# A sequence of four layers on one core: z's high part ahead of the decay, and one tile's y and z a step earlier

## The reference

```
proj = norm(x) @ in_proj_w.T                 # gate (8192), x/B/C (8192 + 2 * 8 * 128), dt (128)
x, B, C = silu(causal_conv(x/B/C, 4 taps));   dt = softplus(dt + dt_bias)
per head h of 128 (64 channels each, 16 heads share a B and a C), in chunks of 128 tokens:
  L[t, s] = exp(cumsum(A dt)[t] - cumsum(A dt)[s]) for s <= t, else 0
  y[t] = sum_s (C[t] . B[s]) L[t, s] dt[s] x[s]  +  exp(cumsum)[t] * C[t] . state(chunk before)  +  D x[t]
y = y * rsqrt(mean(y^2) + eps) * norm_w * silu(gate);   x = x + y @ out_proj_w.T
```

## Time and profile before

| | |
|---|---|
| median of 3 runs | 1723.9 us (1722.81 to 1726.0) |
| the profiled execution | 1723.37 us, span 1721.7 us |
| PE busy | 1668.5 us (97%) |
| ACT, DVE, POOL busy | 1272.1 (74%), 1220.4 (71%), 756.3 us (44%) |
| mean granted clock of PE | 0.989 |
| chain that ended last | PE 80%, DVE 5%, ACT 2% |

### The profile page before, as it was taken

How to read it: one execution, slowest core, us unless ns; L and a number is a source line. 1 busy time by engine, 2 the same in 40 slices (tenths; PEclk the granted TensorE clock), 3 DMA queues, 4 the chain that set the end, 5 groups by cost and what they waited for, 6 DMA issues and landing times.

```text
span 1721.7 us, 27317 instructions
## 1 busy us (share of the span) xinstructions
PE 1668.5 (97%) x9616; PEld 1380.5 (80%) x9616; DVE 1220.4 (71%) x1940; ACT 1272.1 (74%) x2205; POOL 756.3 (44%) x800
## 2 busy tenths in 40 slices
PE   6998898999999999999999999999999999999998
PEld 5877677888888888888888888888888888888777
DVE  6885595767676777677766876776767676767784
ACT  4532249796888688878887888888878888788851
POOL 3662123543444444444444445344444444444570
PEclk9999999999999999999999999999999999999999
DMA  5220325232233233232333332323322323332311
GB/s 190 92 68 1 116 61 166 88 111 80 79 125 106 78 98 113 86 112 87 112 95 110 90 115 87 118 63 119 102 94 94 111 88 105 94 111 76 112 65 49
DMA packets 98567, 166.50 MB, mean 97 GB/s; under 512 B 11616, under 2 KB 49888, under 8 KB 96768
## 3 DMA queue, kind: packets, MB, share of 16 engines
q1 hardware_dynamic: 98432, 164.75, 30.2%
HBM read 158.43 MB, written 6.29 MB: 96 GB/s over the span
## 4 chain that ended last, share of the span: by engine, by line
PE 80%; DVE 5%; ACT 2%; issue 1%; DVEq 0%; ACTq 0%
PE bank L210 15%; PE bank L212 15%; PE bank L211 14%; PE bank L2048 7%; PE bank L2049 7%; PE bank L2014 7%; PE bank L2052 7%; PE bank L2034 4%; PE bank L2000 3%; PE bank L2098 1%; DVE m_xc L1708 1%; DVE m_y L1787 1%; ACT m_mt L1464 1%; DVE m_y L1777 1%; DVE m_gate L1708 0%
## 5 line engine op out<-in xcount | busy, mean ns | idle before, releaser
L210 PE MATMUL bank<-xh,w_h 128*128 128x512 f32 x1152 | 462.6, 402 | 4.2 <-DVE m_xc L1708 3.7
L212 PE MATMUL bank<-xh,w_l 128*128 128x512 f32 x1152 | 452.1, 392 | 0.0
L211 PE MATMUL bank<-xl,w_h 128*128 128x512 f32 x1152 | 448.8, 390 | 0.0
L1372 POOL TENSOR_TENSOR m_z_l<-m_zg,m_z_h 128x512 fp32r<-128x512 f32 x128 | 175.3, 1370 | 514.2 <-ACT m_z_h L1512 514.2
L1464 ACT ACTIVATE m_mt<-m_mt,m_unit 128x128 f32<-128x128 f32 x1024 | 312.2, 390 | 0.0
L1354 POOL TENSOR_TENSOR w_l<-w_raw,w_h 128x512 fp32r<-128x512 f32 x144 | 187.2, 1300 | 248.2 <-ACT w_h L1431 248.2
L1719 DVE TENSOR_TENSOR x<-x,bank 128x512 f32<-128x512 f32 x128 | 87.7, 685 | 248.6 <-PE bank L2052 248.6
L1708 DVE SCALAR_TENSOR_TENSOR m_xc<-bank,m_par_conv,m_xc 128x1020 f32<-128x1020 f32 (+2 forms) x192 | 244.5, 1273 | 14.7 <-ACT m_xc L1443 10.1
L212 PEld LDWEIGHTS bank<-xh,w_l 128*128 128x128 f32 x1152 | 216.4, 188 | 47.9
L210 PEld LDWEIGHTS bank<-xh,w_h 128*128 128x128 f32 x1152 | 217.1, 188 | 46.0 <-issue 5.5
L211 PEld LDWEIGHTS bank<-xl,w_h 128*128 128x128 f32 x1152 | 217.3, 189 | 41.9
(11 more groups left out here) (282 smaller groups left out, 2899.9 us busy)
## 6 DMA issues: line engine op xcount, KB each, us to landing
m_mt<-ncs_rows SPq DMA_DIRECT2D x128, 512.0 KB, 5.1
w_raw<-w_in SPq DMA_DIRECT2D x144, 256.0 KB, 2.7
m_wo_raw<-w_out_in SPq DMA_DIRECT2D x64, 256.0 KB, 4.1
m_e<-ecs_rows SPq DMA_DIRECT2D x128, 128.0 KB, 3.5
a_wo_raw<-wo_in SPq DMA_DIRECT2D x8, 1024.0 KB, 4.9
x<-x_in SPq DMA_DIRECT2D x8, 256.0 KB, 4.3
a_wq_raw<-wq_in SPq DMA_DIRECT2D x8, 256.0 KB, 3.1
x_saved<-x SPq DMA_DIRECT2D x1, 2048.0 KB, 8.8
```

Source lines behind the costliest of these rows:

```text
L210: nc.tensor.matmul(out, ah, bh, start=first, stop=False)
L211: nc.tensor.matmul(out, ah, bl, start=False, stop=False)
L212: return nc.tensor.matmul(out, al, bh, start=False, stop=last)
L1372: nc.gpsimd.tensor_tensor(z_l[:, s % 2, :, :], zg[:], f(z_h[:, s % 2, :, :]), ALU.subtract).then_inc(zl_ready, 1)
```

## The change

Two things are moved, and no instruction is added or removed.

1. In paired steps with t = 1, ACT makes Square and z's high part of tile s - 1 right after `wo_high`, ahead of the decay of tile s + 2.
2. Tile 7 of the last group (`made_last`) gets its y, z, Square, high and low part and its squares' sums at the end of step 7 of that group, its own step, no longer in step 8: on DVE after the mask of tile 9, on ACT after the Silu (ahead of step 8's eviction), on POOL ahead of the x of the chunk's end. SP's load of e for tile 11 moves with it.

```diff
         if not own(kind):
             return []
-        if paired(kind, s):
-            return [s - 1] if behind(kind, s - 1) else []
-        return [s - 1, s] if s == NT else [s]
+        if not paired(kind, s):
+            return [s]
+        return [s - 1] if behind(kind, s - 1) else []
+
+    def made_last(kind, s):
+
+        return kind == "last" and s == NT - 1
...
-                for made in made_in(kind, s):
+                for made in made_in(kind, s) + ([s] if made_last(kind, s) else []):
                     if made % 2 == 1 and ahead(kind, made + 4):
                         sp.wait_ge(y_ready, at(g, made))
                         load_e(g, made + 4)
...
                 for made in made_in(kind, s):
                     split_and_square(g, made)
+                if made_last(kind, s):
+                    split_and_square(g, s)
...
                 if own(kind) and t == 1:
                     for k in range(CT):
                         wo_high(g, half, k)
+                    if paired(kind, s):
+                        square_and_high(g, s - 1)
                 if ahead(kind, s + 2) and not (kind == "lead" and s == STEPS - 1):
                     decay(g, s + 2)
...
-                if paired(kind, s):
+                if paired(kind, s) and t != 1:
                     for made in made_in(kind, s):
                         square_and_high(g, made)
                 for m in EARLY[s]:
                     if has_tile(kind, m) and is_conv[m % TILES]:
                         silu(g, m)
+                if made_last(kind, s):
+                    square_and_high(g, s)
...
                 if ahead(kind, s + 2):
                     mask(g, s + 2)
+                if made_last(kind, s):
+                    make_y(g, s)
+                    make_z(g, s)
```

## The result

| | before | after |
|---|---|---|
| median | 1723.77 us (1722.81 to 1726.0, 5 runs) | 1715.79 us (1715.41 to 1718.02, 5 runs) |
| ratio | | 0.9957, 95% interval 0.9946 to 0.9969 |
| span of the profiled execution | 1721.7 us | 1713.7 us |

The forecast was 1719.0, a gain of 4.9 on the median of then (1723.9), with a range of 1715.5 to 1722.0.

What follows compares the result with a forecast made beforehand. PE was taken as the bound, full from 320 to 1600 us, with two stalls on ACT's high part of z worth removing. Gains of 3.1 + 0 + 1.8 = 4.9 us gave 1719.0 from 1723.9, range 1715.5 to 1722.0.

Steps and rivals of the forecast that it cites:

- no new fall: Rival: PE's clock stays high after the new stalls, weights' low parts in full haste; gain 6.3 to 7.9 us, chance 0.12.
- The two places: PE's stalls in group 0's step 1 and the last group's step 8, with low clock after each: some 10.3 us.
- Tile 0's product: Group 0, step 1: high part ready at 294.5, so the 4.76 us stall and the low clock after it go.
- Tile 1's product: Group 0: starts at 305.35 instead of 310.05 after a new 2.1 us wait for ACT; 4.7 us gained.
- a later product of this group may meet ACT once more: Group 0: without a clock fall, another wait for ACT may follow, so 4.5 us is the upper end there.
- The low clock after that stall: Group 0, tile 1: PE falls to 1.2 GHz after the new wait, costing 1.6 us and leaving 3.1 us.
- the sum: Whole kernel: gains of 3.1 + 0 + 1.8 = 4.9 us.
- The other 14 steps: Other steps with the moved Square: ACT loses 0.4 us inside its 0.53 us idle; nothing reaches PE, 0 us.
- POOL against DVE: Rival: in 15 steps POOL's earlier work slows DVE's low parts, 1.4 us a step; 1738.6 us, chance 0.04 (slower).
- Part 2: Last group, tile 7: stall goes, but PE then waits for the weights' low parts; gain 1.8 us, bounds 0.1 to 3.4.
- DVE's chain: Last group: DVE's work up to the weights' low parts ends at 1618.0 to 1618.5 instead of 1620.14, gaining 1.6 to 2.1 us.

Runs made afterwards that it cites:

- second comparison: The change, unedited, timed again against the kernel before: 1718.49 us (7 runs), ratio 0.9973.
- the third: The change, unedited, timed once more against the kernel before: 1715.24 us (5 runs), ratio 0.9953.
- eviction-first: The change, but in the last group ACT takes step 8's gate eviction ahead of tile 7's Square and high part: 1714.18 us, repeated 1713.77 us.
- part 2 alone: The kernel before with only tile 7 of the last group made in its own step: 1722.31 us (11 runs), ratio 0.9992.
- first-step kernel: The kernel before with Square and high part ahead of the decay only in group 0's step 1: 1717.94 us (12 runs), ratio 0.9971.

## Why the prediction was right, by its own steps

**The number.** The measured time lies inside the range, but only 0.3 us from its lower end, and the gain of 8.0 us lies outside the 3.5 to 6.2 us to which the forecast gave 0.60. What came on PE's path is the case to which it gave 0.12, no new fall, with 6.1 us where that case had 6.3 to 7.9. That the range holds the result is in part luck. The second comparison (4.3 us) lies close to the forecast, the third (8.1) again at the edge. The two places and who holds PE there were right.

**The two places.** Right. One step of 15 holds part 1's whole gain (5.2 us alone, against 0.2 for the 14 others), and the last group holds the rest. The middle windows are unchanged.

**Tile 0's product.** Right: the high part was forecast for 294.5 and stands at 293.99 + 0.62 = 294.6, with no wait of PE.

**Tile 1's product.** Forecast 305.35, found 305.47: 4.6 us gained for 4.7. The stall in front of it was forecast at 2.1 us and is 1.07, because PE came to tile 0's product at 295.52 instead of 294.52. That goes with a stretch at 1.2 GHz ahead of the mixer's first output products. In this profile it lies between 260 and 270 us (mean clock 0.83), and in the seven other profiles with 0.83 there PE is late too, so that the unchanged kernel, once more, stalls for 3.70 us and not 4.76. In the four profiles with 1.00 there, before's among them, PE comes about 1 us sooner. It costs nothing here, since ACT sets the time of tile 1's product either way. Further on "a later product of this group may meet ACT once more": it did, a little: the lead falls from 4.6 us at tile 1's product to 4.3 at tile 3's.

**The low clock after that stall.** This is the term that was mis-sized. I took 1.6 us off for a fall; in this profile there is none. Of two executions with a stall of 1.8 us there, one fell (4.34 us for the 12 products) and one did not (2.86). In all five profiles of the change and of eviction-first the stall was only 1.03 to 1.07 us, and none fell. The forecast of 3.1 for this place became 4.3; without that term the sum would have been 6.3 (with the 4.5 that it names for no fall), against the 6.1 that PE shows.

**The other 14 steps.** 0 us forecast, 0 shown. The slack is thinner than forecast, though. Timelines of ACT, then DVE, in step 1 of group 1, beside the earlier trace rows:

```profile
468.74 0.63 ACT L1515 ACTIVATE m_ysq<-m_y 128x512 f32<-128x512 f32 x1
469.47 0.63 ACT L1518 ACTIVATE m_z_h<-m_zg 128x512 fp32r<-128x512 f32 x1
...
475.01 1.21 ACT L1449 ACTIVATE m_xc<-bank,m_par_conv 128x1024 f32<-128x1024 f32 x1 [0.19 <-PE bank L212]
...
470.74 4.18 DVE L1747 SCALAR_TENSOR_TENSOR m_wo_l<-m_wo_raw,m_par_dn,m_wo_h 128x512 fp32r<-128x512 f32 x4
474.86 2.05 DVE L1762 TENSOR_TENSOR m_mt<-m_mt,m_cb 128x1024 f32<-128x1024 f32 x1
477.80 0.69 DVE L1729 TENSOR_TENSOR x<-x,bank 128x512 f32<-128x512 f32 x1 [0.89 <-PE bank L2065]
```

ACT's idle 0.53 us became 0.19, near the loss of 0.4 that was forecast; Copy's wait for z is 0.2 us of that (469.47 - 468.74 - 0.52). The rival "POOL against DVE" was right in its mechanism: the four low parts take 4.18 us instead of 2.73 in every one of the 14 steps, and the mask 2.05 instead of 1.23 in the step shown. DVE's busy time on the page grows from 1220.4 to 1246.9 us, and none of these 26.5 us reaches PE, since DVE still idles 0.89 us before PE's next tile is done. The forecast had put 1.7 us there and left the mask out.

**Part 2.** 1.8 us forecast, 1.8 found (PE's lead grows from 4.3 to 6.1), by the mechanism named: the late eviction, the late decay, the weights' low parts at 1614.55 and PE waiting 1.95 us for them. The eviction-first kernel shows it from the other side. But the 1.8 is a sum of two terms that were both off. Rows of POOL, ACT and DVE after, whose times are 4.3 us ahead of those in the earlier trace rows:

```profile
1603.42 0.46 POOL L1383 TENSOR_TENSOR m_sq_acc<-m_sq_acc,m_ysq 128x128 f32<-128x128 f32 x1
1603.98 0.63 ACT L1515 ACTIVATE m_ysq<-m_y 128x512 f32<-128x512 f32 x1 [4.07 <-POOL m_sq_acc L1383]
1606.45 1.02 ACT L1457 ACTIVATE m_gate<-bank 128x1024 f32<-128x1024 f32 x1
1614.55 3.63 DVE L1747 SCALAR_TENSOR_TENSOR m_wo_l<-m_wo_raw,m_par_dn,m_wo_h 128x512 fp32r<-128x512 f32 x4
```

On before's time scale POOL's sum of tile 6 is over at 1608.2 and not at 1607.3. That is 0.9 us late, where 0.5 was the bound, while DVE's new y and z run beside it (POOL's first two sums take 1.24 and 0.79 us, before 0.72 and 0.46). The eviction starts at 1610.8 (forecast 1609.8 to 1610.3) and the low parts at 1618.9 (forecast 1618.0 to 1618.5). So DVE's chain gained 1.3 us, less than the forecast 1.6 to 2.1. The four low parts then took 3.63 us instead of the 4.11 that the sum kept, which gave the other 0.5. That the two make 1.8 is luck. A fall of the clock behind the new wait takes two thirds of the gain again, as in part 2 alone.

**The result against the sum.** The spans of the two profiled executions differ by 8.0 us: 6.1 on PE's path plus 1.9 us of a last store that was quick in one profile and slow in the other. Why the medians of the first comparison show the same 8.0 isn't settled. Between the profiles the start of the mixer's first output weights scatters by 2.3 us (A in the table) and the wait for the last stores by 2.1, which together could make the difference between 4.3 and 8.1, but no run here isolates it.

## What to carry to other kernels

Where one engine is full for a whole stretch, look at the few places where it stands still, and follow each repair to the next instruction that is late: here each of the two gave back less than the stall it removed, because the next product met an engine that was only just in time. An instruction that is moved ahead pushes another one back, and what that one was hidden behind counts: the gate's table load was free only while it lay in a wait of ACT, and the change put it behind that wait. Moving two instructions ahead of ten in 14 steps where PE doesn't wait gave nothing and used up most of DVE's slack there (3.10 us idle before its sum, 0.89 after). And where medians scatter by more than the effect, a stretch between two instructions that both kernels share can show it: here the three profiles of the change agree within 0.2 us from A to B.

## What the runs showed of the hardware

- Stalls of PE of nearly the same length were followed by 1.2 GHz in one execution and not in another: 1.83 us (fell) and 1.81 us (didn't), 1.95 us (fell, part 2 alone) and 1.95 us (didn't, the change), and 1.98 us (fell, before) and 1.97 us (didn't until the next tile's product, first-step kernel). The falls cost 1.5 us (first-step kernel) and 1.2 us (part 2 alone). An estimate that takes a fall or leaves it out is off by that much either way.
- Two-input subtractions of DVE from SBUF took 4.18 us for four beside POOL's work, 2.73 alone, and a mask 2.05 instead of 1.23. POOL lost too: the first sum of the squares took 1.24 us beside DVE's y in the last group and 0.72 without it.
- The wait for the last stores of the output came in two sizes, 1.7 and 3.5 to 3.8 us, in profiles of the same kernel.
- A stretch at 1.2 GHz in the experts was there in 8 of 12 profiles and missing in 4. With it the way from B to C took 90.4 us, without it 88.7 to 88.9.
